# Weight pieces of the first expert loop: three output slots, loads two tiles ahead, and the store wait on SP instead of ACT

## The reference

```python
x = x + _L0_conv_ref(_ln_c(x), ...)      # gates, group norm, softmax mixing
t = _to_tokens(x)                         # 4096 tokens x 256
t = t + _L0_ffn_ref(_ln_t(t), ...)        # 8 experts, top 2, H = 512
x = _from_tokens(t, x)
x = x + _L1_conv_ref(_ln_c(x), ...)       # a 1x1 convolution
t = _to_tokens(x)
t = t + _L1_ffn_ref(_ln_t(t), ...)        # 8 experts, top 2, F = 1024
x = _from_tokens(t, x)

# L0_ffn: eo = w2[e] @ (silu(w1[e] x) * (w3[e] x)), weighted by comb
# L1_ffn: y  = silu(x @ w1[e] + b1[e]) @ w2[e] + b2[e], weighted by comb
```

## Time and profile before

| | |
|---|---|
| median of three runs | 1355.62 us |
| the profiled execution's own time | 1357.27 us |
| its span, first to last instruction | 1355.5 us |
| PE busy | 959.7 us, 71% |
| DVE busy | 838.5 us, 62% |
| ACT busy | 562.7 us, 42% |
| POOL busy | 418.1 us, 31% |
| granted TensorE clock, mean of the span | 0.819 of full speed |

### The profile page before, as it was taken

The page is one execution under the profiler, slowest core; times in us unless marked ns, Lnnn a source line. Parts: engine busy times, 40 slices in busy tenths (PEclk is TensorE's granted clock), DMA queues, the critical chain, the costliest instruction groups (busy, mean ns, idle before and its releaser), DMA issues.

```text
span 1355.5 us, 26742 instructions
## 1 busy us (share of the span) xinstructions
PE 959.7 (71%) x7185; PEld 785.9 (58%) x7185; DVE 838.5 (62%) x1909; ACT 562.7 (42%) x1227; POOL 418.1 (31%) x478
## 2 busy tenths in 40 slices
PE   5210386746798887888881088755999999999953
PEld 4100265614676666676661067614888888888842
DVE  6999489897644445445444966593555555555545
ACT  5255323356564454455442013373433443344312
POOL 1385000000144445445442050003443444344410
PEclk8655695557799999999996596556999999999975
DMA  7066105905555655655566701203343442442257
GB/s 249 1 209 209 54 0 173 315 8 154 181 166 168 200 175 173 195 175 177 178 183 213 264 0 46 78 0 86 110 152 87 136 136 77 140 134 75 75 162 251
DMA packets 189007, 188.66 MB, mean 139 GB/s; under 512 B 91232, under 2 KB 158248, under 8 KB 188840
## 3 DMA queue, kind: packets, MB, share of 16 engines
q1 hardware_dynamic: 170616, 145.19, 35.6%
q0 software_dynamic: 14000, 38.82, 8.9%
q10 hardware_dynamic: 4352, 4.20, 0.9%
HBM read 119.46 MB, written 49.28 MB: 124 GB/s over the span
## 4 chain that ended last, share of the span: by engine, by line
PE 39%; DMA 16%; issue 16%; DVE 11%; ACT 6%; SPq 5%; DVEq 2%; POOL 2%; ACTq 1%; POOLq 1%
PE bank L711 15%; PE bank L733 14%; DMA wreg<-in_L_ffn_w_dram 7%; PE bank L644 4%; DMA region<-rows_x,fetch_now 3%; SPq L347 2%; DMA split_v<-wreg 2%; PE bank L561 2%; DMA wreg<-rows_y 2%; ACT xt L883 2%; PE bank L616 1%; ACT wreg L833 1%; POOL rows_y L505 1%; DVE st_lg L996 1%; PE bank L769 1%
## 5 line engine op out<-in xcount | busy, mean ns | idle before, releaser
L711 PE MATMUL bank<-xt,wreg 128*128 x3360 | 384.4, 275 | 20.1 <-DMA xt<-region 17.6
L711 PEld LDWEIGHTS bank<-xt,wreg 128*128 128x128 f16 x3360 | 328.0, 99 | 70.5 <-issue 29.1
L733 PE MATMUL bank<-wreg,region 128*128 128x256 f16 x2520 | 297.9, 276 | 51.3 <-ACT region L912 48.2
L733 PEld LDWEIGHTS bank<-wreg,region 128*128 128x128 f16 x2520 | 239.3, 99 | 103.2 <-ACT region L912 64.0
L505 POOL DMA_INDIRECT rows_y<-region,put_now x140 | 154.6, 1104 | 273.3 <-DVE region L1362 126.4
L917 ACT ACTIVATE region<-bank,b_t,wreg 128x256 f32<-128x256 f32 x280 | 142.1, 561 | 226.7 <-PE bank L711 225.7
L463 POOL DMA_INDIRECT region<-rows_x,fetch_now x144 | 142.9, 993 | 160.5 <-issue 108.2
L1298 DVE SCALAR_TENSOR_TENSOR wreg<-wreg x70 | 49.6, 750 | 181.1 <-ACT wreg L893 178.9
L1354 DVE TENSOR_SCALAR region<-region,wreg 128x512 f16<-128x512 f32 x140 | 76.2, 544 | 73.3 <-ACT region L917 72.8
L561 PE MATMUL bank<-ident,xn 128*128 128x128 f32 x256 | 54.2, 371 | 83.3 <-DVE xn L1005 77.1
L1357 DVE SCALAR_TENSOR_TENSOR region<-region,wreg 128x512 f16<-128x512 f32 x140 | 106.1, 758 | 5.0
(11 more groups left out here) (238 smaller groups left out, 1168.9 us busy)
## 6 DMA issues: line engine op xcount, KB each, us to landing
wreg<-in_L_ffn_w_dram SPq DMA_DIRECT2D x136, 256.0 KB, 3.0
wreg<-in_L_ffn_w_dram SPq DMA_DIRECT2D x48, 512.0 KB, 6.1
split_v<-wreg SPq DMA_DIRECT2D x35, 512.0 KB
wreg<-split_v SPq DMA_DIRECT2D x32, 512.0 KB
wreg<-rows_y SPq DMA_DIRECT2D x48, 256.0 KB, 3.5
rows_x<-region SPq DMA_DIRECT2D x16, 512.0 KB, 3.3
wreg<-in_x_dram SPq DMA_DIRECT2D x4, 1024.0 KB, 9.5
out_dram<-xt ACTq DMA_DIRECT2D x16, 256.0 KB, 3.3
```

The costliest lines, as they stand in the source:

```text
L711: last = pe.matmul(to, block, x_cols[:, bass.ds(b, 1), :, xs_, k, :].rearrange("p j r n -> p (j r) n"), start=(k == 0 and ws_ + xs_ == 0), ...
L733: last = pe.matmul(yb[:, r * C:(r + 1) * C], lhs[:, c, r * P:(r + 1) * P], block, start=first, stop=end, skip_group_check=True)
```

## The change

`piece_out` gets a third slot (the 1024 columns behind it in `wreg` were free in this loop). Pieces 0 and 1 are loaded ahead of the loop, and in turn n of the loop SP loads piece n+2. ACT no longer waits for `piece_stored` before it writes a slot. SP waits for it, together with `piece_loaded` of piece n+1 and `piece_lo` of piece n, ahead of the store of piece n; the load of piece n+2 comes behind the store. `sp_passed` is a semaphore that nobody waits for.

```diff
-        piece_out = wreg[:, 26624:28672].bitcast(F16).rearrange("p (j m s n) -> p j m s n", j=2, m=2, s=2)
+        piece_out = wreg[:, 26624:29696].bitcast(F16).rearrange("p (j m s n) -> p j m s n", j=3, m=2, s=2)
...
@@ store_piece
-                             piece_out[:, bass.ds(n % 2, 1)].rearrange("p j m s n -> p (j m s n)")).then_inc(piece_stored, 16)
+                             piece_out[:, bass.ds(n % 3, 1)].rearrange("p j m s n -> p (j m s n)")).then_inc(piece_stored, 16)
...
@@ turn_tiles
                     sp.wait_ge(w_turned, 6 * E)
                     load_piece(0)
+                    sp.wait_ge(piece_loaded, 32)
+                    load_piece(1)
                 for e in range(E):
                     with sp.Fori(edges[e], edges[e + 1]) as n:
                         sp.wait_ge(z_ready[f], 4 * n + 4)
                         turn_rows(f, n + 2)
                         if f == 0:
-                            with sp.Fori(n, n + 1) as m:
-                                sp.wait_ge(piece_loaded, 32 * m + 32)
-                            load_piece(n + 1)
-                            split = sp.snap(n + 1)
-                            sp.wait_ge(piece_lo, split)
+                            for waited, each, more in ((piece_stored, 16, 0), (piece_loaded, 32, 64), (piece_lo, 1, 1)):
+                                with sp.Fori(n, n + 1) as m:
+                                    sp.wait_ge(waited, each * m + more)
+                                    sp.sem_inc(sp_passed, 1)
                             store_piece(n)
+                            load_piece(n + 2)
...
-            for waited, each, more in ((piece_loaded, 32, 32), (piece_stored, 16, 0), (xc_ready[0][0], 16, 32),
+            for waited, each, more in ((piece_loaded, 32, 64), (piece_stored, 16, 0), (xc_ready[0][0], 16, 32),
...
@@ split_hi (ACT)
                 with act.Fori(n, n + 1) as m:
                     act.wait_ge(piece_loaded, 32 * m + 32)
-                with act.Fori(n, n + 1) as m:
-                    act.wait_ge(piece_stored, 16 * m)
                 for m in range(2):
-                    act.activation(piece_out[:, bass.ds(n % 2, 1), m, 0].rearrange("p j n -> p (j n)"),
+                    act.activation(piece_out[:, bass.ds(n % 3, 1), m, 0].rearrange("p j n -> p (j n)"),
...
@@ split_lo (DVE)
-                    hi, lo = (piece_out[:, bass.ds(n % 2, 1), m, s_].rearrange("p j n -> p (j n)") for s_ in range(2))
+                    hi, lo = (piece_out[:, bass.ds(n % 3, 1), m, s_].rearrange("p j n -> p (j n)") for s_ in range(2))
```

More of the change, by code:

```diff
@@ L264, in bass_metaformer @@
         sum_loaded, summed, peak1_ready = [sem(f"sum_loaded{j}") for j in range(3)], sem("summed"), sem("peak1_ready")
-        v_loaded = sem2("v_loaded")
+        v_loaded, sp_passed = sem2("v_loaded"), sem("sp_passed")
         stage_loaded = sem2("stage_loaded")
```

## The result

The changed kernel takes 1335.3 us (median of 4 runs, 1333.13 to 1337.71) against 1356.43 us for the kernel before in the same runs: ratio 0.9848, 95% interval 0.982 to 0.9877. It is faster, by 21 us or 1.5%; 61 us were forecast, and 1335.3 lies outside the range of 1285 to 1326. The profiled execution took 1337.71 us, span 1336.0 us.

A forecast was written before the change was run, and what follows sets the result against it. The prediction took a two-tile ring through the store to bound the first loop at 10.23 us a tile. Saving 31 x (10.23 - 8.4) = 56.7 us plus 4.3 in the last tile, 61 us, gave 1295 us, range 1285 to 1326.

The forecast's parts named there:

- The store ring: First loop: store, ACT's split, y copy, put, fetch, transposes, loads, next store but one; 19.89 us for two tiles.
- the clock held: PE in the first loop: 0.98 of the clock granted, no loss expected from a denser loop.
- The wait did not simply move to SP: Rival, chance 0.07: SP stands at the store with transposes queued behind it; 10.1 us a tile, 1347 us.
- ring of loads: Rival on SP, chance 0.04: each load issued only after the previous landed; 10.6 us a tile, 1363 us.
- the four rings: First loop, what could bound next: PE 8.14 to 8.27, `y_rows` about 8.3, rows ahead 7.95, `x_rows` 7.5 us a tile.
- PE's pace: First of the four rings: PE's time between `up` starts in early tiles, 8.14 to 8.27 us a tile.
- ring 4: First loop, single `x_rows` buffer: fetch to transposes 3.08, transposes to landed at most 4.4; 7.5 us a tile.
- the first rival: First loop, chance 0.24: DMAs hinder each other, puts take 7.3 us; 9.0 to 9.1 us a tile, 1315 us.
- the `y_rows` ring: First loop, one buffer: y copy end to put 0.95, put landing 6.49, wake 0.1, copy 0.67; about 8.3 us a tile.
- either sign that I gave for a tile over 9 us: First loop: puts landing later than 7.3 us after start, or SP standing at `piece_stored` or `piece_loaded` with transposes behind.
- Behind the loop: After the first loop: SP waits for one more late load; 0 to 1 us, none taken into the sum.
- the rest of the sum: First loop: 31 turns from 10.23 to 8.4 us give 56.7 us, the last tile 4.3; together 61 us.

## Why the prediction was wrong

*Right:* what bounded the kernel before. The store ring is confirmed from two sides, by the kernel that puts the wait back (10.14 us a tile) and by the one that enlarges `x_rows` without the change (10.40). ACT's wait went, PE's wait for ACT went, the clock held, SP never stood at a piece's semaphore, and the load two ahead was early enough (6.8 us of waits in 7 tiles). The wait did not simply move to SP, and no ring of loads formed there. Of the four rings, PE's pace of 8.14 to 8.27 us was right (8.18 with the traffic cut).

*Wrong, the failing step:* ring 4 under "What could close next", "fetch to transposes 3.08, transposes to landed at most 4.4: 7.5 us a tile". The second leg measured 4.4 us. The first was mis-sized: 5.3 us in the turn shown and 5.1 in the median, so the ring is 9.7 us in the turn shown, 9.45 in the medians, and not 7.5, and it, not PE, sets the turn. I took 3.08 us from a fetch that starts at 614.19, when that tile's loads had been out for about 3 us (610.85 and 611.42) and its store for 1.8 (612.36).

What made the difference is when the traffic starts, and both traces show it. In the kernel before, 27 of 33 tiles had their store out at least 1.4 us ahead of the fetch, and both halves then took 4.3 to 5.9 us, 4.9 or less in 24 of them. In the other six the store went out within 1.3 us of the fetch, and it was 5.4 to 6.5 us. In the changed kernel the ring itself fixes the phase: the landing of the transposes releases POOL's fetch 4.4 us behind their start, and SP reaches the store 4.5 us behind the same start (medians). So the store went out within 1 us of the first fetch in 32 of 33 tiles, and in all 32 both halves took 6.1 us or more; the one tile with its store 1.7 us ahead took 5.2. The expectation of the first rival had the right kind of cause (piece traffic in the way of POOL's transfers, 0.24 of chance up to 1338 us) but the wrong buffer: I stretched the put and the `y_rows` ring, and left the fetch at its quiet value. The trace of before held the warning, in a row that I did not use: the early tile whose fetch went out at 389.44 had its transposes only at 393.97, 4.5 us later, with a store issued at 389.73:

```profile
389.73 0.35 SPq L357 DMA_DIRECT2D split_v<-wreg  x1
...
393.97 2.54 SPq L347 DMA_TRANSPOSE xt<-region  x2
```

Put in place of 3.08, it gives 8.9 us a tile and 1311 us, inside the range but still short of what was measured. Nor did either sign that I gave for a tile over 9 us appear: the wait of the y copy for a put was 0.3 us in the whole loop, and SP stood at no semaphore of the piece.

*Wrong, a smaller step:* "Behind the loop ... I put 0 to 1 us on it". It cost 8.4 us. I had SP's last turn at the phase it has in the kernel before, where its transposes start 12.5 us behind the last `up`. In the changed one they start 15.1 us behind it, so the transposes, store and load of work that nobody needs end last. With the traffic cut that way out is 8.9 us long, with two `x_rows` buffers 12.0.

*Wrong, and without consequence:* two readings of rows. The landing times of the earlier trace rows, 3.1 us in the median and 8.5 at worst, belong to loads issued between 18 and 140 us, ahead of the loop; the profile has no landing for the loop's own loads, so no run shows the 3.1 us for them, only that ACT hardly waited for them. And the DMA share does not go with the pace: 0.72 was expected at 8.4 us a tile, and the kernel with two buffers has 0.84 at 8.33.

With the one ring cut, the rest of the sum came close: two buffers give 1294.0 us where 1295 were forecast, with 8.33 us a tile against 8.4. The two numbers agree partly by luck, since 58.8 us come from the turns, 5.1 from the last tile, 2.5 from an earlier start, and 3.3 are lost behind the loop.

## What to carry to other kernels

When a wait is removed, list the rings that are left and size each leg at the phase it will have, not at the one it has now: here a leg that is a DMA grew by half (4.60 to 6.75 us) when 1 MB was issued within 1.5 us of it, and a ring that releases several transfers at nearly the same moment puts them side by side in every turn. Where a transfer comes in halves, count to the last of them. The ring that is one tile long through a single buffer was here the first to close when the pace rose; a second buffer there was worth more (41 us) than the change itself (21 us), and cost 0.7% without it. Loads further ahead and a wait less paid 0.0% and 0.6% alone, 1.5% together.

## What the runs showed of the hardware

- POOL's two gathers of a tile (128 rows of 1 KB each) took 4.37 us, from the first one's start to the transposes that wait for the second, when SP moved 128 KB of pieces in a turn; 5.7 to 5.8 us when it moved 576 KB; 6.75 us when it moved 1 MB, at a DMA share of only 0.68. A mean share below one does not mean that a transfer finds the engines free.
- With the same 1 MB in each turn it took 4.60 us in the median when the store went out 1.7 us ahead of the first gather (the kernel before), and 6.75 us when it went out 0.2 us behind it (the changed kernel).
- The same loop reached a DMA share of 0.84 and 221 GB/s once its ring was cut, so 0.68 was no limit. The share rose faster than the rate: the same 1.8 MB a tile kept the DMA engines busy for 6.0 us at 10.23 us a tile, 6.4 at 9.42 and 7.0 at 8.33.
- Three one-turn loops with their waits met cost SP 1.75 us together with the work ahead of the store (from 616.31, the end of the transposes, to the store at 618.07), two of them 1.33 (loads issued by ACT): about 0.4 us a loop, where I had put 0.3.
